# Cross-attention in two layers: units of 256 queries, and one small step of layer 1 after every small step of layer 0

## The reference

```python
# layer 0: keys 0..1019 are text, the last 4 are image (ip) tokens
scores_t = einsum('bhsd,bhtd->bhst', q, k_t) * attn_scale
probs_t = softmax(scores_t)
text_out = einsum('bhst,bhtd->bhsd', probs_t, v_t)
attn_scores = einsum('bhsd,bhnd->bhsn', q, k_ip) * attn_scale
qsem = _l2norm(einsum('bhst,bte->bhse', probs_t, text_ehs))   # 512 columns for each head
sem = einsum('bhse,bne->bhsn', qsem, _l2norm(ip_ehs))
probs_ip = softmax(attn_scores + 0.5 * sem) * spatial_mask
x = (text_out + probs_ip @ v_ip) @ W_out + b_out + x
# layer 1: keys 0..76 are text, the other 947 ip, each with a softmax of its own
out_text = attend(q, k, v); out_ip = attend(q, k_ip, v_ip)
x = (out_text + out_ip) @ Wo.T + bo + x
```

## Time and profile before

| | |
|---|---|
| median of 3 runs | 3646.05 us (3638.03 to 3647.56) |
| the profiled execution | 3650.53 us, its span 3648.7 us, mean granted clock 0.975 |
| PE busy | 3440.8 us (94%), 21896 matmuls |
| PE weight loads | 2650.6 us (73%) |
| DVE busy | 2018.2 us (55%) |
| ACT busy | 1638.5 us (45%) |
| POOL busy | 824.4 us (23%) |
| DMA | 196.67 MB, mean 54 GB/s |

### The profile page before, as it was taken

The page is one execution under the profiler, slowest core; times in us unless marked ns, Lnnn a source line. Parts: engine busy times, 40 slices in busy tenths (PEclk is TensorE's granted clock), DMA queues, the critical chain, the costliest instruction groups (busy, mean ns, idle before and its releaser), DMA issues.

```text
span 3648.7 us, 58131 instructions
## 1 busy us (share of the span) xinstructions
PE 3440.8 (94%) x21896; PEld 2650.6 (73%) x21896; DVE 2018.2 (55%) x4648; ACT 1638.5 (45%) x3628; POOL 824.4 (23%) x648
## 2 busy tenths in 40 slices
PE   6999999999999999999999999999999999877887
PEld 3788999997888887777777777777688877633333
DVE  4544444453444455655555565655555565656986
ACT  0233434442332345444454454444444554534876
POOL 2111000101101122222222221212221121234665
PEclk8999999999999999999999999999999999988999
DMA  4220111112252111131451111213143111139221
GB/s 157 56 82 25 50 35 28 36 27 82 53 63 71 45 52 50 33 93 36 59 98 43 46 48 50 52 32 88 39 53 37 26 32 33 25 99 79 55 52 33
DMA packets 391741, 196.67 MB, mean 54 GB/s; under 512 B 296972, under 2 KB 355164, under 8 KB 391458
## 3 DMA queue, kind: packets, MB, share of 16 engines
q1 hardware_dynamic: 391464, 192.96, 24.8%
HBM read 136.68 MB, written 55.44 MB: 53 GB/s over the span
## 4 chain that ended last, share of the span: by engine, by line
PE 81%; DVE 6%; ACT 5%; DMA 3%; issue 2%; POOL 2%; SPq 1%; POOLq 0%; ACTq 0%; DVEq 0%
PE acc L783 9%; PE acc L776 9%; PE acc L778 8%; PE acc L779 8%; PE acc L784 8%; PE acc L777 7%; PE av L817 3%; PE spare L853 3%; ACT prob L958 2%; PE spare L817 2%; PE acc L810 2%; PE acc L808 2%; PE score L741 2%; PE score L736 2%; PE score L743 2%
## 5 line engine op out<-in xcount | busy, mean ns | idle before, releaser
L958 ACT ACTIVATE prob<-score 128x512 f32<-128x512 f32 x1280 | 799.4, 625 | 1642.4 <-PE score L743 1241.7
L776 PE MATMUL acc<-tok_v,prob_hi 128*128 128x300 f32 x2240 | 873.4, 390 | 11.8 <-DVE v_f L1083 3.7
L961 ACT ACTIVATE prob_hi<-score 128x512 fp32r<-128x512 f32 x1280 | 799.9, 625 | 0.0
L783 PE MATMUL acc<-tok_v,prob_lo 128*128 128x278 f32 (+1 forms) x2560 | 746.9, 292 | 7.3 <-DVE prob_lo L1021 7.3
L778 PE MATMUL acc<-tok_lo,prob_hi 128*128 128x256 f32 (+1 forms) x2560 | 742.5, 290 | 0.0
L779 PE MATMUL acc<-tok_lo,prob_hi 128*128 128x256 f32 (+1 forms) x2560 | 720.5, 281 | 0.0
L784 PE MATMUL acc<-tok_v,prob_lo 128*128 128x256 f32 (+1 forms) x2560 | 719.5, 281 | 0.0
L1021 DVE TENSOR_TENSOR prob_lo<-prob,prob_hi 128x512 fp32r<-128x512 f32 x880 | 653.0, 743 | 96.7 <-ACT prob_hi L961 95.7
L1255 POOL TENSOR_TENSOR prob_lo<-prob,prob_hi 128x512 fp32r<-128x512 f32 x400 | 529.9, 1338 | 730.5 <-ACT prob_hi L961 729.5
L777 PE MATMUL acc<-tok_v,prob_hi 128*128 128x256 f32 x2240 | 629.2, 281 | 0.0
L778 PEld LDWEIGHTS acc<-tok_lo,prob_hi 128*128 128x128 f32 (+1 forms) x2560 | 485.3, 190 | 10.4 <-issue 9.6
(11 more groups left out here) (221 smaller groups left out, 4438.9 us busy)
## 6 DMA issues: line engine op xcount, KB each, us to landing
k_ring<-k_scr SPq DMA_DIRECT2D x480, 64.0 KB
ctx_t<-in_ctxT SPq DMA_DIRECT2D x8, 2048.0 KB, 10.8
q_ring<-q_scr SPq DMA_DIRECT2D x480, 32.0 KB
v_scr<-v_stage SPq DMA_DIRECT2D x32, 440.0 KB, 2.5
tok_v<-v_scr SPq DMA_DIRECT2D x80, 176.0 KB, 3.3
k_scr<-part_bf SPq DMA_DIRECT2D x32, 384.0 KB, 2.5
v_scr<-v_stage SPq DMA_DIRECT2D x36, 330.0 KB, 9.2
v_ring<-v_scr SPq DMA_DIRECT2D x80, 148.5 KB, 3.3
```

Of the source, the lines that this page charges most:

```text
L776: e.matmul(out_a[:, 0:SEG + VCOLS], p_hi, tok_v[0:kk, c, seg, v_lo:v_lo + SEG + VCOLS], start=first, stop=False)
L783: e.matmul(out_a[:, v_one:v_one + SEG + VH], p_lo, tok_v[0:kk, c, seg, v_lo + v_one:v_lo + v_one + SEG + VH], start=False, stop=False)
L958: e.activation(prob[:, es, :], bank_s[:, :], ACT.Exp, scale=SCALE)
L961: e.activation(prob_hi[:, ps, :], bank_s[:, :], ACT.Exp, scale=SCALE).then_inc(s_exp, 1)
```

## The change

The layers are no longer joined group by group but small step by small step, and units are half as large.

- **Units of 256 queries.** There are 8 units in each layer, each half a batch (`PARTS`). A group has 8 small steps, and 160 groups take the place of 80. A small step of layer 1 is now, like one of layer 0, two key blocks against 256 queries: two score matmuls and four av matmuls of 256 columns (L849, L851, L917, L921). The keys and values of a batch are projected once, for its first unit (`project_kv`), apart from its queries (`project_q`). Maxima stay 1280 matmuls; `max_rows` comes 160 times and not 80, with the same 3 or 6 DMAs each.
- **One step of layer 1 after each of layer 0.** After 124 small steps of layer 0 alone (`LAG_UNITS`), each small step of layer 0 is followed by one of layer 1, 515 times; 125 of layer 1 are left at the end ("tail").
- **Banks.** One score bank (`score0`) serves both layers until the tail; the other, and `spare`, serve the background. Layer 1 sums in `av0`, a bank of its own. Scores are issued one pair of steps ahead.
- **prob_lo.** In the woven part POOL computes all those of layer 1, DVE those of layer 0.
- **Loads and maxima.** The ring has 5 places. q and k of a group are loaded 24 small steps ahead of its start (32 in the tail), not groups ahead; with 8 small steps a group the DMAs of k double, since each half batch loads the keys again. SP issues 3726 DMAs in place of 1966. The maxima of a woven group are spread over small steps start-19 to start-8; the step `max_rows` is split into the negation (`neg`) and, two small steps later, the transposition and what follows. The group's first score stands a pair ahead of its products.
- **The start.** Only the first third of q and k is projected before the first score; the maxima of two groups of 256 queries come before it in place of those of one group of 512.

```diff
-RING = 4
-LOOK_MAX = 2
-LOOK_LOAD = 3
+RING = 5
...
-LAYER_LAG = 17
-WEIGHT = (4, 1)
+LAG_UNITS = 124
+WINDOW = 4
...
-AHEAD = 3
-P_SLOTS = AHEAD + 1
-LOW_LAG = 1
+P_SLOTS = 4
...
+MAX_SPAN = {"lead": (8, 5), "woven": (11, 8), "tail": (8, 11)}
+BATCHES, PARTS = 4, 2
+B, SQ, D, E, T = BATCHES * PARTS, 512 // PARTS, 320, 512, 1024
...
+    for i in range(total + LAG_UNITS):
+        if i < total:
+            add(0, i)
+        if i >= LAG_UNITS:
+            add(1, i - LAG_UNITS)
...
+        def neg_task():
+            o.add("neg", g)
+            if rest:
+                urgent.append((now[0] + rest, rows_task))
...
+            at = max(end_of[g - RING], start_of[g] - (24 if start_of[g] < tail else 32))
...
+        span, margin = MAX_SPAN[phase(start_of[g])]
+        last_at = start_of[g] - margin
+        first_at = max(last_at - span, loads_from.get(g, -4) + 4, latest_at.get(UNITS[seq[g][0]][0], 0))
...
+            following = next_upper.get(n, n + 2)
+            score_to(following)
+            for k in range(2):
+                o.add("mix", n, 0, k)
+                hook(1 + (len(topq) + len(bgq)) // 8)
+            if following + 1 < len(chunks) and UNITS[chunks[following + 1][1]][0] == 1:
+                score_to(following + 1)
...
+            low_to(following)
...
+            for k in range(2):
+                o.add("mix", n, 1, k)
+                hook(1 + (len(topq) + len(bgq)) // 8)
...
-    on_pool = [layer_of[n] == 1 and n % 8 in (0, 2, 3, 5, 6) for n in range(len(chunks))]
+    on_pool = [layer_of[n] == 1 and (n < tail or n % 8 in (0, 2, 3, 5, 6)) for n in range(len(chunks))]
...
+    score_name = ["score0" if n < tail + 3 or (n - tail) % 2 else "acc1" for n in range(len(chunks))]
...
+            name = "acc0" if n >= tail and h % 2 else "av0"
...
-                    if n >= 2:
-                        e.wait_ge(s_exp, n - 1)
-                    if UNITS[u][0] == 1:
-                        e.matmul(score[n % 2][:, :], k_ring[0:depth, slot, j, c * P:(c + 1) * P],
-                                 q_ring[0:depth, slot, j, :], start=True, stop=True).then_inc(s_score, 1)
...
+                    if score_before[n] >= 0:
+                        e.wait_ge(s_exp, score_before[n] + 1)
...
-                    e.matmul(both[0:n_out, :], weights, prob_hi[:, ps, :], start=first, stop=False, skip_group_check=not first)
+                    for k in range(UNIT_KEYS):
+                        e.matmul(both[0:n_out[k], 0:SQ], weights[k], prob_hi[:, ps, queries[k]],
+                                 start=r == 0 and k == 0, stop=False, skip_group_check=r > 0 or k > 0)
                     e.wait_ge(s_low[on_pool[n]], low_nth[n])
```

More of the change, by code:

```diff
@@ L191, in load_v, with maxima @@
         o.add("load_v", g)
-    def maxima(g):
+    def maxima(g, rest=2):
         def half_task(j, st, half):
@@ L311, in plan @@
     run_all(*first_v[0:5])
-    rest, top = first_v[5:], maxima(0)
+    rest, top = first_v[5:], maxima(0, rest=0) + maxima(1, rest=0)
     while rest or top:
@@ new lines, in plan, with score_to, low_to @@
+    scored, lowered = [-1], [-1]
+    def score_to(n):
+        while scored[0] < min(n, len(chunks) - 1):
+            scored[0] += 1
+            g = chunks[scored[0]][0]
+            while g not in rows_done:
+                if not (current or topq or bgq or urgent and urgent[0][0] <= now[0]):
+                    forced.append((now[0], g))
+                    urgent[0] = (now[0], urgent[0][1])
+                run_step()
+            o.add("score", scored[0])
+    def low_to(n):
+        while lowered[0] < min(n, scored[0]):
+            lowered[0] += 1
+            o.add("low", lowered[0])
@@ new lines, in rows_of, with hook @@
+    def rows_of(n):
+        _, u, h, c = chunks[n]
+        if n < 0 or UNITS[u][0] == 0 or c < NU - 1:
+            return
+        o.add("l1_rows", n)
+        urgent.append((n + 3, lambda: turn_head(u, h)))
+        if h == HEADS - 1:
+            urgent.append((n + 3, lambda: unit_done(u)))
+    def hook(limit):
+        while later and later[0][0] <= now[0]:
+            later.popleft()[1]()
+        slot_no[0] += 1
+        for _ in range(limit):
+            if not current:
+                due = bool(urgent and urgent[0][0] <= now[0])
+                if not due and not topq and not bgq or slot_no[0] < rest_until[0] and len(topq) + len(bgq) + due < BACKLOG:
+                    return
+            run_step()
+            if not current:
+                rest_until[0] = slot_no[0] + SPACING
@@ L809, in _ @@
+                    for k in range(UNIT_KEYS):
+                        e.matmul(both[0:n_out[k], 0:SQ], weights[k], prob_hi[:, ps, queries[k]],
+                                 start=r == 0 and k == 0, stop=False, skip_group_check=r > 0 or k > 0)
                     e.wait_ge(s_low[on_pool[n]], low_nth[n])
-                    e.matmul(both[0:n_out, :], weights, prob_lo[:, ps, :], start=False, stop=first or last, skip_group_check=not first).then_inc(s_main, 1)
+                    for k in range(UNIT_KEYS):
+                        mm = e.matmul(both[0:n_out[k], 0:SQ], weights[k], prob_lo[:, ps, queries[k]], start=False,
+                                      stop=r == 0 and k == 0 or r == NU - 1 and k == 1, skip_group_check=r > 0 or k > 0)
```

769 lines of the change are left out of this document (403 added, 366 removed).

## The result

The changed kernel takes 3930.52 us (median of 4 runs, 3926.09 to 3935.86) against 3644.1 for the one before in the same comparison: a ratio of 1.0789, 95% interval 1.0766 to 1.0812. It is slower by 286 us. The forecast was slower by 63, 3709 us, with a range to 3800: the sign was right, the size was not.

The account below looks back on a forecast made before the run. PE's own stream was taken to bound the kernel, except in the last stage. Terms 0 + 33 - 268 + 198 - 55 + 135 + 20 = +63; 3650.5 + 63 - 4.5 = 3709 us, range 3560 to 3800.

Parts of the forecast that it names:

- Rows of maxima: First scores of groups before and in the weave: PE waits for late row DMAs, +135 us (75 to 228).
- rival B: Row DMAs on SP's queue are issued at .46 us each, as loads are: 3643 us; chance .13.
- Rival C, the late queue: SP's queue late as a whole; half of 130 woven groups lose 1.5 us more: +100, 3809 us; chance .15.
- A: Rival: rows come in time, as DMAs of one set overlap in their cost: 3591 us; chance .17.
- The clock after waits: PE at reduced clock after six new waits of about 6 us, 3.4 us each: +20 us; shorter waits 0.
- Waits for prob_lo: PE's 60.9 us idle at L810 before both layers' end mostly goes: -55 us.
- The tail: Last stage: 125 small steps in place of 288, 221 us against 489: -268 us.
- Narrower matmuls: Layer 1: 512-column matmuls split into 256 columns, 27 us, plus 80 more transpositions, 6 us: +33 us.
- what moves: 163 small steps and the last batch's K and V projections move from the last stage under layer 0: +198 us.
- One score bank: Woven part: each score's wait for the exponential before it is hidden by .2 us: 0, up to +40.
- The start: Before the first score: about 10 us of q and k projections leave and return under layer 0: 0.
- My two signs of being wrong altogether: The tail stays above 300 us, or the woven stage has waits by DMA of loads, put at nothing.

Follow-up runs that it names:

- experiment 2: Changed kernel with 1050 more score matmuls of 256 columns filling the waits before 61 first scores of woven groups: 3895.58 us, 1.0690.
- experiment 10: Kernel before with only the negation split off, transposition and what follows two small steps later: 3673.18 us, 1.0091.
- experiments 1: Changed kernel with maxima earlier: woven over 9 small steps ending 11 ahead of the group's start, before the weave ending 7 ahead: 3795.73 us, 1.0418.
- the sixth experiment: Changed kernel with three places for layer 1's values, woven maxima 20 to 11 small steps ahead, the tail's 22 to 14: 3753.95 us, 1.0299.
- experiment 3: Kernel before with each 512-column score and product matmul of layer 1 split in two of 256 columns: 3642.91 us, .9994.
- experiment 7: The sixth experiment with the 960 DMAs that load q issued by ACT and not by SP: 3980.42 us, 1.0917.
- experiment 8: Changed kernel with woven prob_lo of layer 1 on POOL for 5 of 8 small steps, the rest on DVE: 3919.78 us, 1.0758.

## Why the prediction was wrong

- **Rows of maxima, +135.** Mechanism right, size low: 166 us before the tail, and 22 more in it. The DMAs were priced well (.63 us each, not .46: rival B is out; in the chain shown the last lands 1.2 us after its issue ended). What was missing: DVE's part took 2.3 us on average from the transposition in the woven stage (1.9 before), and 14 sets before the tail came 51 us late in sum behind other DMAs on SP's queue, 46 of them time in which SP was issuing. Rival C, the late queue, was thus a part of it and not a case by itself; A is out.
- **The clock after waits, +20: the worst step of the stages before the tail.** It measured +78. I charged only the six longest waits at 3.4 us each. There were 10 of 5 us or more, but most of the half clock stands at waits of 1.7 to 4.5 us (experiment 2), which I had put at 0. The row was there, and I used it as a price for rare events though my own count of distances forecast some 50 waits; there were 74.
- **Waits for prob_lo, -55: a misread row.** The earlier trace rows sum the idle time of PE's matmuls and of its weight loads at L810, which wait beside each other for the same thing. PE's own waits there are 29.9 us over the whole kernel (fence in experiment 10), 19 of them in the stage in question. So 19 could go, and did: -36 us of the forecast never existed. The check was at hand, as the whole stage has 61 us without a busy PE, which I took for agreement.
- **The tail, -268.** It measured -205. These are its parts (columns as in the earlier trace rows): until the last 80 small steps, those, and the end.

```profile
3650.00:3766.30 116.30, 71.42 (x371) 45.43 (x369) 67.01 (x185) 50.23 (x101) 37.66 (x31) 0.75 0.25 57
3766.30:3914.90 148.60, 107.74 (x636) 71.83 (x637) 111.80 (x287) 86.83 (x180) 67.79 (x52) 0.80 0.23 45
3914.90:3934.00 19.10, 11.72 (x32) 6.00 (x29) 6.59 (x19) 0.38 (x1) 0.00 (x0) 0.56 0.13 38
```

The forecast had 103, 98 and 20. The stall of the last unit's queries (10.6 us for 10) and the end were right; the step that failed is the 80 steps at 1.22 us, the old stage's pace at its fastest, where they took 1.86. What was missing is that half as many queries need as many DMAs, now for each 9.8 us of steps: values, rows and first loads come late (waits of 25, 22 and 15 us in the tail), and PE, idle a third of the time, spends 133 of 284 us at half clock. I had "at worst +11" for the queue and nothing for the clock. Wider margins and the third place for values took 31 us off (experiments 1 and 6).
- **Narrower matmuls, +33, and what moves, +198**: 231 forecast, 239 measured (some 255 by the stricter charge for the clock), by luck in part: the narrow matmuls cost nothing (experiment 3), the rest was more than I counted.
- **One score bank, 0**: 8.4 us of waits. Right, with the thin cover that experiment 7 shows.
- **The start, 0**: -6, which the table counts in its first rows.

Sum of the misses: 26 for rows (31, less 5 that the first rows cost before), 36 for prob_lo, 30 for other new waits (maxima for a bank or for DVE, above all), 58 for the clock, 9 for work, 63 for the tail: 222 us, which is 285 less 63. My two signs of being wrong altogether didn't come: the tail is 284 us long, and the profile puts no wait of PE in the woven stage down to a load. They were too loose. Of the narrower ones the tail (210 to 240 us) and PE's busy time until the last mix (3217 us, where it is 3317) missed.

The largest error stands above the single steps. Before, all that any reordering could win was 208 us of idle time and 92 of clock; the other 3348 are PE's work. The tail's 489 us looked like the prize, but 352 of them were work. It could bring the forecast's net 268 - 198 = 70 us only if nothing new waited.

## What to carry to other kernels

Sort the span of the bounding engine into work, idle and half clock before pricing a reordering: only the last two can be won, and a short low-use stage may hold little of either. When units are halved, everything that is paid once per unit (DMAs in one in-order queue, a chain through three engines) must fit in half the time, and a prefetch distance counted in steps halves too. Charge the expected waits of PE with the clock behind them, also those of 2 to 5 us. What stays open: no run has small steps woven with units of 512 queries, or halved units without the weave, so what each of the two costs alone isn't shown.

## What the hardware showed that I had not expected

DVE's small steps of the row chain are stretched while POOL computes a prob_lo. L1258 and L1262 take .28 us alone and 1.25 to 1.40 where POOL's 1.3 us operation covers nearly 90% of them (27 cases in the changed kernel); the cast L1256 takes .21 alone and .75 on average under it, though 8 of 30 stay at .21; the reductions from PSUM (L1231, L1233) stay at .60 and .68 either way. The rows of 1462.86 and 1463.03 above show it once: DVE's .28 us step ends .15 us after POOL's. DVE's prob_lo goes from .68 to .85 on average where the two overlap.

This is not what made the woven stage slower. There it adds .27 us to a set of rows, against .20 in the same stage before, and with 5 of 8 prob_lo on POOL (experiment 8) 31 of 129 sets are stretched in place of 32. The rest of DVE's 2.3 us is that DVE starts .63 us after the transposition and not .31. It counts in experiment 10, where it adds 1.2 us to a set in the last stage (.14 before), and in the changed kernel's tail, where it adds 1.3 and DVE's part takes 4.4 us.

A DMA issued by ACT isn't free for ACT: 960 of them, .45 us each, with their waits, put 193 us of waits for prob_hi on PE where the sixth experiment has 9.
